# Two buffers for the pieces of queries and keys, another DRAM layout, six operand loads in place of twelve

## The reference, cut to what matters

```
x = (inputs @ W_qkv + b_qkv).reshape(Bv, HEADS, Sv, -1)
q, k, v = jnp.split(x, 3, axis=-1)
qk = jnp.einsum('bhse,bhte->bhst', q, k) * scale
attn = jax.nn.softmax(qk + mask, axis=-1)
sa = jnp.einsum('bhst,bhte->bhse', attn, v).reshape(Bv, Sv, -1)
return sa @ W_out + b_out
```

## Time and profile before

| | |
|---|---|
| median of 3 runs | 816.09 us (815.59 to 817.51) |
| the profiled execution | 818.8 us, span 816.9 us |
| PE busy | 706.8 us, 87% of the span |
| DVE, ACT, POOL busy | 549.5, 403.6, 382.2 us |
| DMA | 92.49 MB, mean 113 GB/s; SP's queue 58.5% of 16 DMA engines |
| wait of ACT's first piece for the pieces' store | 37.7 us in 8 places |

### The profile page before, as it was taken

One profiled execution on the slowest core, in us unless ns is written; L12 is line 12 of the kernel. 1 busy time (PEld: TensorE's weight loads), 2 busy tenths in 40 slices (PEclk: granted clock), 3 DMA queues, 4 the chain that ended last, 5 costly groups with the idle time before them and its releaser, 6 DMA issues. The chain is left out here.

```text
span 816.9 us, 12493 instructions
## 1 busy us (share of the span) xinstructions
PE 706.8 (87%) x3987; PEld 305.7 (37%) x3987; DVE 549.5 (67%) x1562; ACT 403.6 (49%) x908; POOL 382.2 (47%) x774
## 2 busy tenths in 40 slices
PE   4886997959989988979879896989999889988996
PEld 2443553313323322313222231323333237756655
DVE  4563786879979996959768694969999102454401
ACT  2231222718667765747566563757667661212330
POOL 5328403455667665545555545554532341235313
PEclk9998999979999998979989797989999898988999
DMA  8857774888779769569393757548542404652012
GB/s 279 217 141 155 195 189 128 144 138 145 130 125 153 124 86 142 76 96 118 70 155 49 123 71 99 81 66 138 72 44 27 119 3 112 193 183 91 7 19 26
DMA packets 252945, 92.49 MB, mean 113 GB/s; under 512 B 213760, under 2 KB 233376, under 8 KB 252832
## 3 DMA queue, kind: packets, MB, share of 16 engines
q1 hardware_dynamic: 251344, 89.60, 58.5%
q0 software_dynamic: 1536, 2.10, 1.6%
HBM read 56.65 MB, written 35.01 MB: 112 GB/s over the span
## 5 line engine op out<-in xcount | busy, mean ns | idle before, releaser
L1216 DVE CUSTOM_DVE_ANT_0 ps<-ps,maskrow 128x640 f32<-128x640 f32 (+7 forms) x512 | 375.6, 779 | 63.8 <-PE ps L949 61.4
L822 ACT ACTIVATE strips<-ps 128x512 f32<-128x512 f32 (+1 forms) x608 | 311.0, 577 | 138.0 <-PE ps L969 128.0
L969 PE MATMUL ps<-QTq,QTk 99*128 99x512 bf16 (+3 forms) x768 | 197.1, 346 | 48.3 <-ACT strips L822 31.8
L949 PE MATMUL ps<-QTk,QTq 96*128 96x512 bf16 (+3 forms) x768 | 194.8, 343 | 18.0 <-DVE mx L1216 12.6
L987 PE MATMUL ps<-strips,vext 128*32 128x512 f32 (+3 forms) x1536 | 170.7, 524 | 1.5 <-POOL strips L1623 1.0
L969 PEld LDWEIGHTS ps<-QTq,QTk 99*128 99x128 bf16 x768 | 69.5, 100 | 144.7 <-ACT strips L822 79.2
L949 PEld LDWEIGHTS ps<-QTk,QTq 96*128 96x128 bf16 x768 | 54.7, 100 | 176.2 <-DVE mx L1216 131.6
L1623 POOL TENSOR_SCALAR_AFFINE_SELECT strips<-strips 128x512 f32<-128x512 f32 x128 | 79.7, 637 | 75.8 <-ACT strips L822 75.4
L917 PE MATMUL ps<-shared,xrT 128*128 128x384 f32 (+1 forms) x256 | 96.0, 514 | 0.0
L1216 DVE DVE_READ_ACCUMULATOR2_ANT mx<- 128x1 f32 x512 | 72.4, 141 | 0.0
L1517 POOL TENSOR_TENSOR r<-qkT,pieces 128x1024 f32<-128x1024 f32 x16 | 34.1, 2131 | 64.7 <-ACT pieces L801 64.7
(11 more groups left out here) (146 smaller groups left out, 695.9 us busy)
## 6 DMA issues: line engine op xcount, KB each, us to landing
qkv_d<-shared SPq DMA_DIRECT2D x32, 384.0 KB, 3.1
pieces_d<-pieces SPq DMA_DIRECT2D x16, 768.0 KB, 8.9
QTq<-pieces_d SPq DMA_DIRECT2D x96, 128.0 KB, 4.5
QTk<-pieces_d SPq DMA_DIRECT2D x96, 128.0 KB, 6.9
qk<-qkv_d SPq DMA_DIRECT2D x64, 128.0 KB, 4.1
vext<-qkv_d SPq DMA_DIRECT2D x16, 256.0 KB, 6.1
sa_d<-pmo SPq DMA_DIRECT2D x64, 64.0 KB, 3.1
QTq<-sa_d SPq DMA_DIRECT2D x8, 512.0 KB, 5.4
```

The costliest lines, as they stand in the source:

```text
L822: nc.scalar.activation(dst, src, ACT.Exp, scale=SCALE).then_inc(exp_done, 1)
L949: mm = pe.matmul(psM[:, s, at:at + n], QTq[0:W, f % 3, c * 1024 + qb * P:c * 1024 + (qb + 1) * P], QTk[0:W, f % 3, c * 1024 + k0:c * 1024 ...
L969: mm = pe.matmul(psE[:, (NE * q + j) % ES, k * n:(k + 1) * n], QTk[0:W + 3, q % 3, c * 1024 + kb * P:c * 1024 + (kb + 1) * P], QTq[0:W + 3 ...
L1216: ins = nc.vector.tensor_tensor_reduce(scores, scores, maskrow[:, 1024 - n:1024], 1.0, MASKED, ALU.add, ALU.max, mx[:, f % 2, 8 * c + qb:8 ...
```

## The change

- `pieces` has two buffers, by f % 2, with a semaphore each. `first_piece(f)` waits for the store of f - 2.
- `pieces_d` is [step, query or key, 16, piece, 4, 1024]: the four blocks of 1024 of one row and piece lie together, 8 KB. A store is four transfers, one for each 32 partitions, in runs of 2 KB.
- `TERMS` is reordered so that equal pieces of the query come in runs of three, two and one. A load takes a whole run: for the queries one piece, broadcast to 3, 2 or 1 copies, for the keys pieces 0 to n - 1. Six loads of 48, 32 and 16 partitions in rows of 8 KB take the place of twelve, in two parts.
- In the planner stores and loads are two chains. Durations and landing times are new, and the first score products are due a little earlier (1.5 steps ahead for 1.34). The order of every engine comes out anew.

```diff
-TERMS = ((0, 2), (0, 1), (0, 0), (1, 0), (2, 0), (1, 1))
+TERMS = ((0, 0), (0, 1), (0, 2), (1, 0), (1, 1), (2, 0))
+RUNS = ((0, 3), (3, 2), (5, 1))
...
-        ("Sync", "STORE"): [x for f in range(2, STEPS) for x in (("STORE", f), ("LOAD", f, 0), ("LOAD", f, 1), ("LOAD", f, 2))],
+        ("Sync", "STORE"): [("STORE", f) for f in range(2, STEPS)],
+        ("Sync", "LOAD"): [("LOAD", f, part) for f in range(2, STEPS) for part in range(2)],
...
-                return latest(after(("Vector", ("TP", x[1]))), done.get(("landed", ("STORE", x[1] - 1))) if x[1] > 2 else 0.0)
+                return latest(after(("Vector", ("TP", x[1]))), done.get(("landed", ("STORE", x[1] - 2))) if x[1] > 3 else 0.0)
...
-            return STEP * (x[1] - 1.34 + (NU * x[2] + x[3]) / (4 * NU))
+            return STEP * (x[1] - 1.5 + (NU * x[2] + x[3]) / (4 * NU))
...
-        pieces_d = nc.dram_tensor("pieces_d", [NQ, P, 3, 1024], BF16).ap()
+        pieces_d = nc.dram_tensor("pieces_d", [NQ, 2, D, 3, 4, 1024], BF16).ap()
...
-        pieces = sb("pieces", [P, 3, 1024], BF16)
+        pieces = sb("pieces", [P, 2, 3, 1024], BF16)
...
-                sp.dma_start(pieces_d[f], pieces[:, :, :]).then_inc(pieces_st, 16)
+                for c in range(4):
+                    sp.dma_start(pieces_d[f][:, :, :, c, :].rearrange("y d k n -> (y d) k n"),
+                                 pieces[32 * c:32 * c + 32, f % 2, :, :]).then_inc(pieces_st[f % 2], 16)
...
-                    sp.wait_ge(pieces_st, 16 * (f + 1))
+                    sp.wait_ge(pieces_st[f % 2], 64 * (f // 2 + 1))
                     if f >= 3:
                         sp.wait_ge(qk_ps, NE * (f - 2))
-                rows = pieces_d[f].rearrange("(c y d) k n -> y k d c n", c=4, y=2)
-                for n in range(4 * part, 4 * part + 4):
-                    y, i = n // len(TERMS), n % len(TERMS)
-                    operand = (QTq, QTk)[y][D * i:D * (i + 1), f % 3, :].rearrange("d (c n) -> d c n", c=4)
-                    sp.dma_start(operand, rows[y, TERMS[i][y]]).then_inc(qk_in[f % 3], 16)
+                for i, n in RUNS:
+                    operand = (QTq, QTk)[part][D * i:D * (i + n), f % 3, :]
+                    if part == 0:
+                        rows = pieces_d[f, 0, :, TERMS[i][0]].rearrange("d c n -> d (c n)")
+                        src = rows.unsqueeze(0).to_broadcast([n, D, 4096])
+                    else:
+                        src = pieces_d[f, 1, :, 0:n].rearrange("d k c n -> k d (c n)")
+                    sp.dma_start(operand, src).then_inc(qk_in[f % 3], 16)
...
-                if f > 0:
-                    act.wait_ge(pieces_st, 16 * f)
-                nc.scalar.activation(pieces[:, 0, :], qkT[:, :], ACT.Copy).then_inc(p1_done, 1)
+                if f > 1:
+                    act.wait_ge(pieces_st[f % 2], 64 * (f // 2))
+                nc.scalar.activation(pieces[:, f % 2, 0, :], qkT[:, :], ACT.Copy).then_inc(p1_done, 1)
...
-                        pe.wait_ge(qk_in[f % 3], 16 * 2 * len(TERMS) * (f // 3 + 1))
+                        pe.wait_ge(qk_in[f % 3], 16 * 2 * len(RUNS) * (f // 3 + 1))
```

More of the change, by code:

```diff
@@ L78 @@
 TENSOR = {"ST": 0.25}
-VECTOR = {"TP": 1.2, "MXT": 0.25, "OT": 0.68, "OREC": 0.17, "R": 0.3, "S": 0.6, "ST": 0.2, "SMAX": 1.2}
+VECTOR = {"TP": 1.17, "MXT": 0.15, "OT": 0.65, "OREC": 0.18, "R": 0.36, "S": 0.8, "ST": 0.2, "SMAX": 1.2}
 SCALAR = {"P1": 1.1, "RX": 0.5, "R": 0.25}
-GPSIMD = {"SPLIT": 5.8, "MAX": 1.2, "CAUSAL": 0.72, "RA": 1.6, "S": 2.9, "ROUTES": 1.8, "SA": 0.65}
-SYNC = {"LQK": 2.0, "LV": 0.6, "STORE": 0.6, "LOAD": 2.0, "LM": 1.5, "SA": 2.0, "S_OUT": 0.5, "S_IN": 3.0, "BULK": 4.0}
-LANDS = {"LQK": 9.0, "LV": 8.0, "STORE": 4.0, "LOAD": 8.0, "LM": 2.5, "SA": 6.0, "S_OUT": 2.5, "S_IN": 3.0, "BULK": 12.0}
+GPSIMD = {"SPLIT": 5.5, "MAX": 1.2, "CAUSAL": 0.68, "RA": 1.6, "S": 2.9, "ROUTES": 1.8, "SA": 0.65}
+SYNC = {"LQK": 2.6, "LV": 0.6, "STORE": 1.9, "LOAD": 1.4, "LM": 3.2, "SA": 2.4, "S_OUT": 0.5, "S_IN": 3.0, "BULK": 4.0}
+LANDS = {"LQK": 7.0, "LV": 6.0, "STORE": 5.0, "LOAD": 8.0, "LM": 2.0, "SA": 5.0, "S_OUT": 2.5, "S_IN": 3.0, "BULK": 12.0}
 def product_time(n):
@@ L128, in schedule @@
     for f in range(2):
-        done["landed", ("LOAD", f, 2)] = done["landed", ("LV", f)] = 0.0
+        done["landed", ("LOAD", f, 1)] = done["landed", ("LV", f)] = 0.0
     def after(*keys):
@@ L146, in ready @@
             if kind == "C":
-                return latest(slot_free(), done.get(("landed", ("LOAD", x[1], 2))))
+                return latest(slot_free(), done.get(("landed", ("LOAD", x[1], 1))))
             if kind == "E":
@@ L255, in takes @@
             widths = [(qb + 1) * P for qb in UNITS[x[3]]]
-            return sum(product_time(n) if engine == "Tensor" else 0.12 + n / 960 for n in widths)
+            return sum(product_time(n) if engine == "Tensor" else 0.117 + n / 960 for n in widths)
         if kind == "PV":
@@ L511, in layer_kernel @@
         piece_done = sem("piece_done")
-        pieces_st = sem("pieces_st")
+        pieces_st = [sem(f"pieces_st{u}") for u in range(2)]
         qk_in = [sem(f"qk_in{b}") for b in range(3)]
@@ L667, in _ @@
                     store_pieces(0)
-                elif t in (11, 12, 13):
+                elif t in (11, 12):
                     load_pieces(0, t - 11)
@@ L675, in _ @@
                     load_qk(2)
-                elif t in (20, 21, 22):
-                    load_pieces(1, t - 20)
+                elif t in (19, 20):
+                    load_pieces(1, t - 19)
             def store_sa(q):
@@ L1516, in split @@
                     pool.wait_ge(piece_done, 3 * f)
-                pool.tensor_tensor(r1[:, :], qkT[:, :], pieces[:, 0, :], ALU.subtract).then_inc(piece_done, 1)
+                pool.tensor_tensor(r1[:, :], qkT[:, :], pieces[:, f % 2, 0, :], ALU.subtract).then_inc(piece_done, 1)
                 pool.wait_ge(piece_done, 3 * f + 1)
-                pool.tensor_copy(pieces[:, 1, :], r1[:, :]).then_inc(piece_done, 1)
+                pool.tensor_copy(pieces[:, f % 2, 1, :], r1[:, :]).then_inc(piece_done, 1)
                 pool.wait_ge(piece_done, 3 * f + 2)
-                pool.tensor_tensor(pieces[:, 2, :], r1[:, :], pieces[:, 1, :], ALU.subtract).then_inc(piece_done, 1)
+                pool.tensor_tensor(pieces[:, f % 2, 2, :], r1[:, :], pieces[:, f % 2, 1, :], ALU.subtract).then_inc(piece_done, 1)
             def maxima(f):
```

## The result

| | before | after |
|---|---|---|
| median of 4 runs | 815.84 us (813.08 to 817.51) | 968.21 us (965.66 to 971.9) |
| ratio, with its 95% interval | | 1.1875 (1.1823 to 1.1927) |
| span of the profiled execution | 816.9 us | 970.1 us |
| granted clock, mean | 0.928 | 0.867 |

Slower by 152 us. The forecast was 899 us, 83 more than before, and the upper end of its range 968. The direction and the mechanism were right; three sizes in the sum were too small.

What follows compares the result with a forecast made beforehand. DMA, not PE, was to set the attention steps: 485 - 6 + 55 + 30 = 564 us where 502 were, +62; with +21 in front, 818.8 became 901.8, less 2.7 gives 899 us, range 845 to 968.

Steps and rivals of the forecast that it cites:

- upper end: Top of the forecast range, 968 us: a set at 20.8 GB/s per DMA engine, 4.3 us more for each of 16 sets.
- (c) Outermost counts decide: Operand loads: the outermost count sets how many DMA engines serve a load, so three for n = 3, two for n = 2.
- The rival that leaned on "Rules for kernel authors": Operand loads: all sixteen DMA engines take part and the 37.7 us of waits end, 33 us gained, 783 us; chance 0.11.
- The set's price, 22.9 us: All operand loads of one attention step: 22.9 us on the busiest DMA engine, where it cost 11.2.
- The rest of a step's transfers, 164 us, less 6 for the last step: Attention part's qk, v, sa, m and pieces transfers: 164 us of each DMA engine, less 6 for the last step without a set.
- The empty 4.2 us of each step, 55 us: Attention part, around the m store: 4.2 us empty on the busiest DMA engine, no longer covered; thirteen steps, 55 us.
- Front, +21: Front part, sets 0 and 1 between qkv stores: 10.5 of each set's 11.7 us growth, +21 us (ends 0 and 23).
- The end, 0: The end of the kernel, from 667 us on, holds no set: 0 us change.
- Two buffers worth nothing here: Attention part: two buffers and stores taken out of the loads' chain give nothing, as DMA sets the steps.
- the waits of 37.7 us end: ACT's first piece waiting for the pieces' store, 37.7 us in 8 places: ends, as the piece before last was stored earlier.
- Late next is the m store: Attention part: the m store is late next, waiting for loads and v behind them; no separate size given.
- What would show it: Signs in the profile after: DMA share near 0.2, 50 to 75 GB/s, steps of 35 to 40 us, one over 50.

Runs made afterwards that it cites:

- experiment 1: The changed kernel with each operand load cut into its terms, twelve loads of 16 rows of 8 KB: 792.08 us, ratio 0.962 to the kernel before.
- experiment 11: The changed kernel's same six loads with the 16 rows outermost in the source in place of the copies or terms: 782.84 us, ratio 0.954 to the kernel before.
- experiment 5: The changed kernel with operand load sets 0 and 1 cut to one load per term, later sets unchanged: 946.02 us, ratio 1.165 to the kernel before.
- experiment 12: The kernel before with the planner's part alone (one buffer, old layout, one store, twelve loads, due time 1.5): 774.86 us, ratio 0.947.
- experiment 7: The changed kernel with one buffer for the pieces in place of two: 976.58 us, ratio 1.200 to the kernel before.
- experiments 9: The changed kernel with one load per term and one buffer for the pieces: 780.38 us, ratio 0.953 to the kernel before.
- experiment 3: The changed kernel's two buffers and planner order, with the DRAM layout, one store and twelve loads of the kernel before: 790.22 us, ratio 0.965.
- 8: The changed kernel with the planner's due time back at 1.34 steps ahead in place of 1.5: 988.71 us, ratio 1.217 to the kernel before.
- 10: The changed kernel with one load per term, two buffers and the due time back at 1.34 steps: 809.71 us, ratio 0.988 to the kernel before.

## Why the forecast was right and where it was wrong

**Which step failed.** The mechanism held; the prices in its sum did not. Three terms were too small. A set was put at 22.9 us and took 26.3 on average. All other transfers of the attention part were put at 164 us of each DMA engine, with nothing for the stores in packets of 2 KB; the packet records have 184 before and 194 after. The front part was put at +21 and grew by 32.7. The upper end, 968, varied the set's rate alone; that it lies so near the measured time is luck, since the sets averaged less than the 27.2 us that it took, and other terms made up the rest.

**(c) Outermost counts decide: right, and now shown.** Experiments 1 and 11 hold layout, bytes and row length fixed, and 11 the number of loads as well; counts of 3 and 2 give 968 us, a count of 16 gives 783. The rule of the Trainium skill that the forecast cited (DMA: Bandwidth & Descriptors, "Why a DMA increments its semaphore by 16 and not by 1"), on its case of 3 against 48, was not shown by a row then; experiment 11 and the tail at two sixteenths of the DMA share agree with it. Only two streams are left at the end, after 66 rows' worth of time, so both narrow kinds share their DMA engines; that these are the lowest-numbered, no record here shows. The rival that leaned on "Rules for kernel authors" of that page, sixteen engines and 783 us, is refuted for the change as written. It is what the loads give once the 16 rows are outermost.

**The set's price, 22.9 us: too low.** In the packet records of the set at 496 us the rows run from 497.9 to 523.3 us: 25.4 us for 66 rows on the busiest DMA engine, 385 ns each. In the tail, with two streams, a row takes 312 ns, better than the 329 ns that the forecast took from the w1h load; at the start of the set, with three streams and other transfers between them, rows of 600 to 900 ns occur. The value I took had the long stretch's rate for the whole set. Of the 14 sets of the attention part, 12 took 25.2 to 26.8 us, and the two whose halves were issued apart 29.5 and 28.6: 368 us in all, where the forecast had 321. That is +47 us.

**The rest of a step's transfers, 164 us, less 6 for the last step: too low.** With 368 us of sets, 50 us without any packet in the fourteen steps with a set, and a last step of 30 us, 620.6 leaves 173 us for the other transfers, where the forecast had 158. That is +15 us. The number is a remainder, not a measurement, and part of the other transfers ran inside the sets' 368. The packet records measure the term itself, as a mean over the sixteen DMA engines. Before, the packets of the 14 sets took 153 us (10.9 a set, where the forecast took 12.3 from one stretch), so the others had 184, not 164. After, they have 194, and the growth is mostly the stores of the pieces: their packets of 6 KB took 31 us, those of 2 KB take 46. That was put at nothing ("they stand in the same 164"). The remainder also holds what the busiest DMA engine lost in other ways, such as SP held in an issue while that engine ran dry. Those held issues were foreseen (over 10 us), but not priced; there are twelve in the attention part, of 14 to 19 us each.

**The empty 4.2 us of each step, 55 us: nearly right, 50.** The packet records show 10.7 us with no packet on any DMA engine in the first step and 2 to 4 us in each of the next thirteen. The forecast counted thirteen steps with a set; fourteen lie between the first and the last m load.

**Front, +21: too low, 32.7.** Of these 28.0 belong to the two sets (experiment 5). Two sets of 25.8 and 25.2 us instead of 11.2 make 28.6. So all of the growth came through, and the slack that I still granted the stores of qkv was none; DVE's wait for them went from 3.2 to 30.3 us. The other 4.7 us I put down to the new order, which had no term in the sum; with the planner's part alone (experiment 12) the first m load is at 143.9 us, 5.8 later than before.

**The end, 0: right** (+1.4). The sum is then 62 + 47 + 15 - 5 = 119 for the attention part, 33 in front and 1 at the end.

**Two buffers worth nothing here: right, with a wrong reason for more.** With one buffer the median of the change is 8 us higher, not clear of noise (experiment 7). But that "the waits of 37.7 us end" was reasoned from the buffer ("the piece before last was stored a step earlier"), and there it was wrong: with wide loads and one buffer they end as well (1.3 and 1.7 us in experiments 9 and 12). What ended the waits was not the buffer but the planner's part: the store's place in SP's chain ahead of the loads, the due time and the new durations. Which of the three does it wasn't separated. No experiment shows a gain from the second buffer under wide loads: 0.962 and 0.965 with two (1 and 3), 0.953 and 0.947 with one (9 and 12). These pairs ran in different sessions; only for the old layout do the intervals lie apart. In the trace of experiment 3 one and a half sets lie between the m loads of steps 3 and 4, a step of 40 us, as the planner runs ahead with two buffers, and in that of 12 the same step takes 33. Whether this is the whole difference wasn't tried.

**The due time: left out of the sum altogether.** "A little earlier" got no term. It is worth some 20 us under narrow loads (8) and about as much under wide ones (10 against 1: 0.988 and 0.962, so 21 us). In both, of PE's waits for transfers the one for the m load grows most without it: 54.3 us in 8 where the change has 32.7, and 26.8 in 10 where experiment 1 has 12.2.

**Late next is the m store: half right.** PE waited 32.7 us for the m load, but 76.4 us for the operands themselves, which I had not named.

**What would show it:** share near 0.2 (0.12 to 0.30, but 0.70 while the v load and a qk load run beside the set), 50 to 75 GB/s (52 to 72, and 102 there), one early step of over 50 us (two of them: 65.8 and 63.5), others of 35 to 40 (30 to 48), issues held over 10 us, the last load of a set landing over 21 us after its issue (the operands were complete after 27.6), no wait for the store: seen. When the first load of three copies landed, which was to be some 7 us after its issue, the views don't give.

## What to carry to other kernels

Before joining loads, write down the outermost count of both sides of each: a broadcast or a stack of pieces put outermost turned a 1.5 MB set from sixteen streams into two or three, and swapping two dimensions gave back 185 of 968 us. Measure a change's parts alone before believing in any: here the planner's part by itself gave 5.3%, while the loads it was shipped with cost 22% (968 for 792 us), and no gain from the buffer was seen. When a wait names a buffer, look first at what its release is queued behind; the planner's new order removed the wait without a second buffer. And give every term of a sum its own ends: a range that varies one rate alone is too narrow when three terms are off the same way.

## What the runs showed of the hardware

- One DMA engine writing rows of 8 KB to SBUF took 312 ns a row (26 GB/s) with two active. With twelve one-term loads on sixteen engines a row of 8 KB took some 970 ns (median over the sets of experiment 1), so 16 x 8,192 B / 0.97 us = 135 GB/s in all, near the 140 of the earlier trace rows with runs of 2 KB: the longer runs bring nothing there. With the 48-, 32- and 16-partition loads of experiment 11 a row took some 670 ns, and a stretch of the set moved 188 GB/s, shared with other transfers.
- Behind a set on few DMA engines, SP's own issue stops: one qk load of 128 KB was held for 17.88 us, while at the set's end fourteen of the DMA engines had nothing to do (share 0.126). Twelve issues were held for 14 to 19 us in the attention part, and everything behind them in SP's order waited.
- The granted clock fell after PE stood still: PE was idle from 514.9 to 523.9 us, and from 517.6 to 527.8 the clock was at 0.50 (1.2 GHz, where it is 2.4 at 1.00). So the first 3.9 us of work after the wait ran at the lower level.
- The mean was 0.84 in the attention part for 0.92, and 0.71 in its first step. The work of the part is the same, but PE's busy time in it rose from 440.9 to 458.9 us; in experiment 12, at 0.95, it was 425.2. How much of that reaches the end of the kernel wasn't separated from the waits.
